# The last phase of a two-layer block on one Trainium2 core: the second layer's bias goes to another engine, the final sum to another place in the slot

## What is computed

```
x = x + conv(ln_c(x))          # conv: depthwise 3x3, 1x5, 5x1, then a 1x1 (pw), times its normalised input
t = to_tokens(x)               # 96 channels per token
t = t + ffn(ln_t(t))           # ffn: fp8 inputs, W1 96 -> 384, relu, fp8, W2 384 -> 96
x = from_tokens(t)
# inside ffn, with q_acc rounding to 10 mantissa bits (float16):
h = relu(q_acc(q_acc(q_mul(x) @ q_mul(W1).T) + q_mul(b1)))
y = q_acc(q_acc(q_mul(h) @ q_mul(W2).T) + q_mul(b2))     # the bias b2 is the one that moves
```

## Time and profile before

| what | us |
|---|---|
| median of 3 runs | 3661.55 (3657.33 to 3664.26) |
| the profiled execution, its own time | 3659.49 |
| its span, first to last instruction | 3657.6 |
| busy in the span: PE, DVE, ACT, POOL | 3017.4, 3218.4, 2781.3, 1728.9 |
| phase C, from the first mix at 2562.85 to the end | 1094.8 |

### The profile page before, as it was taken

How to read it: one execution, slowest core, us unless ns; L and a number is a source line. 1 busy time by engine, 2 the same in 40 slices (tenths; PEclk the granted TensorE clock), 3 DMA queues, 4 the chain that set the end, 5 groups by cost and what they waited for, 6 DMA issues and landing times. The chain is left out here.

```text
span 3657.6 us, 68122 instructions
## 1 busy us (share of the span) xinstructions
PE 3017.4 (82%) x21990; PEld 1910.0 (52%) x21990; DVE 3218.4 (88%) x8131; ACT 2781.3 (76%) x6274; POOL 1728.9 (47%) x2404
## 2 busy tenths in 40 slices
PE   6787888878787878887876799997888888888887
PEld 5565665656565656565654344443444444444444
DVE  4888889898989898989886699999899999999998
ACT  2577777777777877777778455554799999999998
POOL 3777777777787877787864000000222222222221
PEclk9999999899999999999987899999999999999999
DMA  3233323232323232323212888897676667666762
GB/s 68 53 89 74 91 71 88 71 88 70 88 71 88 71 88 71 88 71 88 71 56 69 212 238 234 236 280 212 172 199 188 181 185 200 184 184 193 199 177 83
DMA packets 696178, 478.92 MB, mean 131 GB/s; under 512 B 407217, under 2 KB 674422, under 8 KB 683830
## 3 DMA queue, kind: packets, MB, share of 16 engines
q1 hardware_dynamic: 695830, 474.58, 49.2%
HBM read 272.09 MB, written 201.92 MB: 130 GB/s over the span
## 5 line engine op out<-in xcount | busy, mean ns | idle before, releaser
L1891 POOL TENSOR_SCALAR C_var<-C_st 128x16 f32<-128x16 f32 x64 | 13.5, 211 | 1338.6 <-DVE C_st L178 1338.6
L1464 DVE SCALAR_TENSOR_TENSOR B_y<-B_mid,B_coefs,B_y 128x512 f32<-128x512 f32 x768 | 509.0, 750 | 3.2 <-ACT B_y L1429 3.2
L1395 PE MATMUL B_ps_row<-B_z,B_band 128*128 128x512 f32 x1152 | 499.1, 596 | 15.1 <-DMA B_band<-edge_scratch 15.1
L378 DVE TENSOR_SCALAR A_hq<-A_h,A_b 128x512 f16<-128x512 f16 x768 | 319.4, 456 | 176.5 <-ACT A_h L370 169.6
L370 ACT ACTIVATE A_h<-A_hid 128x512 f16<-128x512 f32 x768 | 428.3, 594 | 59.5 <-PE A_hid L357 57.1
L178 DVE BATCH_NORM_STATS2 A_st<-A_xT 128x6 f32<-128x192 f32 x1536 | 443.6, 349 | 29.3 <-ACT A_xT L861 16.0
L370 ACT ACTIVATE C_h<-C_hid 128x512 f16<-128x512 f32 x768 | 425.0, 589 | 22.9 <-PE C_hid L357 22.5
L1504 ACT ACTIVATE C_q<-C_xT,C_shift,C_rstd 128x96 fp8e5<-128x96 f32 x1024 | 392.6, 457 | 43.3 <-POOL C_shift L1898 43.2
L894 ACT ACTIVATE A_xc<-A_xT,A_shift,A_rstd 128x96 f32<-128x96 f32 x1024 | 379.3, 456 | 4.2 <-POOL A_shift L1207 4.0
L167 POOL TENSOR_TENSOR A_rstd<-A_var,A_expo 128x16 f32<-128x16 f32 x128 | 376.5, 2941 | 10.7
L1395 PEld LDWEIGHTS B_ps_row<-B_z,B_band 128*128 128x128 f32 x1152 | 218.8, 190 | 294.2 <-issue 287.8
(11 more groups left out here) (167 smaller groups left out, 7248.7 us busy)
## 6 DMA issues: line engine op xcount, KB each, us to landing
A_xq<-in_x SPq DMA_DIRECT2D x32, 1536.0 KB, 8.9
x_scratch<-A_xT SPq DMA_DIRECT2D x64, 768.0 KB, 3.2
x_scratch<-A_x3h SPq DMA_DIRECT2D x64, 768.0 KB, 5.4
B_z<-x_scratch SPq DMA_DIRECT2D x96, 512.0 KB
y_scratch<-B_y SPq DMA_DIRECT2D x96, 512.0 KB, 3.6
C_x3q<-x_scratch SPq DMA_DIRECT2D x32, 1536.0 KB, 9.1
C_xT<-x_scratch SPq DMA_DIRECT2D x64, 768.0 KB, 16.6
C_y3q<-y_scratch SPq DMA_DIRECT2D x31, 1536.0 KB, 15.6
```

The lines of the kernel that those rows point to most:

```text
L378: r = dve.tensor_scalar(self.hq[:, b, s], self.h16[:, b, s], self.w["b1"][:, j:j + 1], 0.0, ALU.add, ALU.max)
L1395: m = pe.matmul(bank(c, h), band[c.buf(NB)][:, d, :], z[c.buf(NB)][:, half(h), d:d + W], start=(d == 0), stop=(d == 2))
L1464: dve.scalar_tensor_tensor(y, mid[c.buf(2)][:, half(h), t:t + W], coefs[:, c.n, 3 + t:4 + t], y, ALU.mult, ALU.add).then_inc(ev["sums"], 1)
```

## The change

Two things. The bias of the second layer, 256 instructions of 96 x 512 float16, goes from DVE to POOL (`pool_y`, with a wait on `out`, since POOL now writes a buffer that DVE reads). And DVE's `out` of group k is issued in slot k + 2 instead of at the end of slot k + 1, right behind `dve_hidden` and ahead of `gate`; out(7) goes to slot 0 of the next step. POOL's stream now goes through the slots: y of each group, and `norm_terms` behind y(3) and y(7).

```diff
-    def dve_y(self, dve, i, k):
+    def pool_y(self, pool, i, k):
         ev = self.ev
 
-        dve.wait_ge(ev["y16"], ev.at("y16", i, k))
-        dve.tensor_scalar(self.y16b[:, k % 2, :], self.y16[:, k % 2, :], self.w["b2"][:, 0:1], None,
-                          ALU.add).then_inc(ev["yb"], 1)
+        pool.wait_ge(ev["y16"], ev.at("y16", i, k))
+
+        if k >= 2:
+            pool.wait_ge(ev["out"], ev.at("out", i, k - 2))
+        elif begun(i - 1):
+            pool.wait_ge(ev["out"], ev.at("out", i - 1, NK - 2 + k))
+        pool.tensor_scalar(self.y16b[:, k % 2, :], self.y16[:, k % 2, :], self.w["b2"][:, 0:1], None,
+                           ALU.add).then_inc(ev["yb"], 1)
...
             def body(i):
-                q = i + 1
+                q, p = i + 1, i - 1
                 for s in range(FFN_SLOTS):
                     if i.real and s < NK:
                         ff.dve_hidden(dve, i, s)
+                    if s == 0 and p.real:
+                        out(p, NK - 1)
+                    if i.real and s >= 2:
+                        out(i, s - 2)
                     if q.real and s < NK:
                         gate(q, s)
                     if q.real and s >= 1:
                         x4(q, s - 1)
-                    if i.real and s >= 1:
-                        ff.dve_y(dve, i, s - 1)
                     if q.real and s >= 1:
                         stats(q, s - 1)
-                    if i.real and s >= 1:
-                        out(i, s - 1)
 
             steps(dve, body)
+            out(Unit(0, NQ - 1, 4, NQ - 1), NK - 1)
...
             def body(i):
                 q = i + 1
-                for half in range(2):
-                    if q.real:
-                        norm_terms(q, half)
+                for s in range(1, FFN_SLOTS):
+                    if i.real:
+                        ff.pool_y(pool, i, s - 1)
+                    if q.real and s % 4 == 0:
+                        norm_terms(q, s // 4 - 1)
```

## The result

The changed kernel takes **3746.8 us** (median of 4 runs, 3746.1 to 3750.0) against 3662.2 (4 runs of the kernel before): a ratio of **1.0235, 95% interval 1.0217 to 1.0252**. It is slower, as forecast, but by 85 us where 60 was the sum, and 5 us beyond the upper end of the range. The span of the profiled execution grew from 3657.6 to 3744.0.

The account below looks back on a forecast made before the run. ACT (3.95 us a slot) or DVE (3.83) sets the beat, just above a three-engine loop of 3.58 that the change lengthens. 31 units x 1.83 = 57, + 3 = 60 on 3659.5: 3719 us, range 3697 to 3742.

Parts of the forecast that it names:

- The loop through gate and mix, 4.17: L382, gate, mix, hidden part 2, h2, next L382: the moved out adds 0.59 to 3.58, giving 4.17 us a slot.
- The bank, 4.28: PE's turn in slots 3 to 6 waits for out's bank, making the loop 4.28 us over four distances.
- The seam without POOL, +0.4: Slot 7 to slot 1: out(6) starts 2.67 and up to 0.1 more after L382(7) instead of 2.34, about +0.4 us.
- the absorbed 0.35: ACT's 0.35 us wait for POOL before normalising group 4 absorbs the seam's delay, leaving +0.05 a unit.
- The bias on POOL, 0.8 us, bounds 0.76 and 1.13: POOL's bias instruction takes 0.8 us, from small rows; at the upper bound 1.13 it adds 8 us in all.
- A slot and a half to spare, so it is hidden, but for one place: out(k) needs POOL's bias a slot and a half later; only y(7), ahead of the second norm_terms, could delay anything.
- Rival (c): POOL's bias takes 1.5 us, norm_terms starts 0.7 later, 0.65 a unit reaches ACT: 20 more, 3739 us; chance 0.13.
- Rival (d): POOL's bias blocks DVE's relus, 0.3 us for each group of three: 77 more, 3796 us; chance 0.04.
- The last unit, 3 us: No gate or mix there, but the bank's wait and POOL's longer bias ahead of the last store: 3 us added.
- (a): Faster: DVE's relief counts and the loop does not, gaining 1.0 a unit, 31 in all: 3628 us; chance 0.08.
- (b): No difference: the turn's wait is hidden and the loop costs about what the bias returns, 3660 us; chance 0.04.
- A sign that was wrong: DVE's busy time was to be down by 256 x 0.34 = 88 us, with more idle before the relus.

Follow-up runs that it names:

- e1: The changed kernel with the bias back on DVE, so that only the move of out remains: 3722.4 us, ratio 1.0160.
- e3: The changed kernel with POOL adding the bias to 32 of the 512 columns only: 3720.8 us, ratio 1.0154.
- e4: The changed kernel with the four back banks dealt out by use (one q8, one y, two c), so no turn waits for out: 3755.6 us, ratio 1.0252.
- e6: Against e1 (bias on DVE), out one place further back, behind gate instead of ahead of it: 3785.8 us, ratio 1.0347.
- e12: The changed kernel with POOL's bias written as a two-input addition, the bias column repeated along the row: 3730.1 us, ratio 1.0194.
- e2: The kernel before with only the bias moved to POOL, out staying at the end of its slot: 3847.4 us, ratio 1.0503.

## Why the prediction was right in direction and short in size

- **The loop through gate and mix, 4.17.** Right: 4.18 from slot 6 to 7 in e1 and e3, and 4.18 from slot 2 to 6 in e4, where the bank is out of the way.
- **The bank, 4.28.** Right: 4.27 in the four distances named in e1 and e3 (in the changed kernel in three, the fourth is 4.39), PE idle 0.89 before the turn; e6 confirms the same 0.78 from out to turn on a path 0.6 longer.
- **The seam without POOL, +0.4, and the absorbed 0.35.** Nearly: 6.58 in e3 against 6.52, and the distance from 1 to 2 fell from 4.41 to 3.95 rather than 4.06. Together within 0.05.
- **The bias on POOL, 0.8 us, bounds 0.76 and 1.13.** This is the step that failed, and in the sum it was priced at nothing, as hidden. The instruction takes 1.56, outside both bounds, and costs the 26 us between the changed kernel and e3. I carried the slope between two small shapes to a size eight times as large, and took the two-input rows for the more expensive form, hence for an upper end; on this chip, at 512 elements, the one-input form is the slower one (1.485 with a constant, 1.035 for two inputs). "A slot and a half to spare, so it is hidden, but for one place" failed with it: at 1.56 out(6) waits 0.36, and y(4) reaches into relus and L382. The length is not the whole of the failure: at 1.035, inside the bounds, e12 still took 3730.1. The prediction gave 3728 for its upper end, but by a norm_terms that starts late; in e12 the loss is a relu held up beside y(4), so that the two figures agree is luck.
- **Rival (c)**, a slow POOL, had the right size of the instruction (1.5) and nearly the right time (3739), but another mechanism: norm_terms did start 0.68 late (5.62 after L382(7), 4.94 before), but the later seam covered that, and ACT's wait for it is gone; the loss is at out(6) and L382.
- **Rival (d)**, POOL blocks DVE, holds at the one place named for it, y(4) behind norm_terms, where the sum had put no price: 0.1 + 0.3 a unit, some 12 us. By the rule of the Trainium skill cited in the prediction ("SBUF — State Buffer", section "Who interferes with whom") the second to issue is blocked for the whole of the first. The trace of e12 agrees: a relu that started 0.01 after POOL's two-input instruction ended 0.15 after it. The trace of the changed kernel agrees only in part: L382, issued at 2862.78, ends 0.41 after POOL's one-input instruction does, but the second relu, issued 0.01 after that one, ends 0.74 before it, and the third runs inside it in its usual 0.34. Together the delays cost 0.4 a unit, not 1.5. In e3 the long instruction is gone and the longest relu is 408 ns. Nor was y(4) the only meeting: the first relu of slots 3 to 5 takes 0.49 beside the end of POOL's bias (0.35 alone), but the last relu waits for ACT there, and nothing is lost.
- **The last unit, 3 us.** From its first L382 to the end it takes 4.5 longer, and 4.2 longer in e3. So the bank and the loop cost more here than the 3, and POOL's length little, though the last two sums wait 0.94 and 1.73 for it. Right in kind.
- **(a) and (b)**: DVE's relief gave nothing: e1 with the bias on DVE and e3 with nearly none are 1.6 us apart. DVE's idle before the relus grew from 49.0 to 112.3 us.
- **A sign that was wrong:** DVE's busy time was to fall by 88 us. It rose, from 3218.4 to 3237.0: the bias had cost 0.26 each from start to start and not 0.34, and what overlapped or ran at its own length before no longer does.

The sum, in which POOL's bias costs nothing, was 3719; e3, where POOL's bias is nearly gone, took 3720.8. The range was drawn around the wrong place for POOL: (c) belonged in the middle.

## What to carry to other kernels

Moving an instruction later on an engine that is nearly full looks free when its result is not urgent; follow instead every buffer it frees and every instruction that now stands behind it. Here a sum that nobody waited for held a PSUM bank and stood ahead of a gate, and each set a slower beat of its own: 4.18 with the gate alone (e4) and 4.87 with the bank alone (e6, where out starts 0.60 later), against 3.95. An operation that the trace does not show at its own size and form has no price from small rows: run it, or carry a wide bound (here it was twice what the small rows gave), and give a price to each place where it runs beside another engine's work. The gain lay in two instructions of DVE swapped at the one place a unit where a chain of another engine was waiting.

## What the runs showed of the hardware that I had not expected

- On POOL a one-input addition of 96 x 512 takes 1485 ns with a constant and 1560 with a column, in float16 and in float32 alike; a two-input addition of the same size 1035. At 32 columns the one-input form takes 359.
- Beside POOL's two-input instruction of 1.03 us a relu of DVE took 1.18 and ended 0.15 after it. Beside the one-input instruction of 1.56 a relu took 0.81 and ended 0.74 before it, and the next one took its usual 0.34. In turn POOL's bias, 1.56 otherwise, reached 2.03 in the changed kernel.
- The granted clock of TensorE in a stretch of 300 us of phase C was 1.00 in the changed kernel and 0.93 in e2, where it idles for up to 3.5 us before mix; in e4 it was 0.62 in the four microseconds behind a wait of 1.71, and the same three matmuls took 1.49 instead of 0.81.
